# The second layer's head: x added to the latent products by PE, sigmoids from PSUM, and copies by ACT in place of DVE's sums

## What is computed

```python
base = sigmoid(r) * (num / maximum(den, 1e-8)); out = base * (0.8 + 0.2 * tf)     # r is x
...
x_lat = x @ fc1_w.T                                       # layer 0: 32 small experts in a space of 128
h = relu2(einsum('tl,eil->eti', x_lat, w1)) * cw.T[:, :, None]
routed = einsum('eti,eli->tl', h, w2) @ fc2_w.T
...                                                       # out = shared + routed
X1_q = rows quantized by their absmax; X2 = gelu(X1_q @ W1_q.T * scales + B1)     # layer 1
out = quantized(X2) @ W2_q.T * scales + B2
```

## Time and profile before

| | |
|---|---|
| three runs | 461.81, 463.07, 463.24 us; median 463.07 |
| the profiled execution | 462.28 us, its span 460.5 us |
| busy, share of the span | PE 89%, PEld 57%, DVE 72%, ACT 53%, POOL 52% |
| mean granted clock of PE | 0.974 |
| 181 to 199 us | end of layer 0's experts, head of layer 1 |
| 199 to 229 us | layer 1's loop over 8 tiles |
| 235 to 247 us | routing of layer 2 |
| 254 to 401 us | layer 2's 23 blocks of experts |

### The profile page before, as it was taken

One profiled execution on the slowest core, in us unless ns is written; L12 is line 12 of the kernel. 1 busy time (PEld: TensorE's weight loads), 2 busy tenths in 40 slices (PEclk: granted clock), 3 DMA queues, 4 the chain that ended last, 5 costly groups with the idle time before them and its releaser, 6 DMA issues.

```text
span 460.5 us, 6031 instructions
## 1 busy us (share of the span) xinstructions
PE 408.4 (89%) x1734; PEld 261.8 (57%) x1741; DVE 329.3 (72%) x621; ACT 243.5 (53%) x486; POOL 240.8 (52%) x339
## 2 busy tenths in 40 slices
PE   7798999999899999777765999999999999985795
PEld 7576787555455556445632456665556666652553
DVE  5997789999999998899765277547547311028995
ACT  6534682667667667568963132333323232328884
POOL 5473036686789995232003457866775454204642
PEclk9999999999999999979995799999999999999999
DMA  7900006356555543000025878898899986050011
GB/s 227 407 11 0 1 1 227 128 189 221 184 200 171 216 168 137 1 1 2 1 91 174 319 273 289 297 370 288 331 343 311 311 305 216 31 186 0 13 36 46
DMA packets 23664, 77.39 MB, mean 168 GB/s; under 512 B 3440, under 2 KB 7920, under 8 KB 20176
## 3 DMA queue, kind: packets, MB, share of 16 engines
q1 hardware_dynamic: 20336, 69.94, 42.7%
q0 software_dynamic: 2208, 6.03, 4.3%
q10 hardware_dynamic: 1088, 1.05, 0.7%
HBM read 71.76 MB, written 5.24 MB: 167 GB/s over the span
## 4 chain that ended last, share of the span: by engine, by line
PE 35%; issue 5%; DVE 4%; ACT 4%; DMA 3%; POOL 1%; ACTq 0%; POOLq 0%; DVEq 0%
PE bank L1957 18%; PE bank L1977 10%; PE bank L1968 2%; DVE gl L1543 2%; PE bank L1940 1%; DMA gy<-y_rows 1%; PE bank L1827 1%; DMA xb<-cond_rows,row_i 1%; DVE pt L1550 1%; PE bank L1808 1%; PE bank L1819 1%; ACT q2T L838 1%; POOL st L623 1%; DMA y_rows<-yb,dest_i 1%; ACT gl L830 0%
## 5 line engine op out<-in xcount | busy, mean ns | idle before, releaser
L1957 PE MATMUL bank<-gu,xbT 128*128 128x512 f32 x184 | 86.0, 612 | 0.9 <-ACT xbT L903 0.9
L1739 PE MATMUL bank<-hx,w2raw 128*128 128x512 f32 x128 | 67.2, 607 | 4.2 <-DVE hx L1278 3.3
L1479 DVE TENSOR_TENSOR hm<-bank,sl 128x512 f32<-128x512 f32 x23 | 15.9, 692 | 71.3 <-PE bank L1957 40.3
L781 ACT ACTIVATE rl<-bank 128x512 f32<-128x512 f32 x64 | 38.1, 595 | 37.9 <-PE bank L1586 37.1
L1957 PEld LDWEIGHTS bank<-gu,xbT 128*128 128x128 f32 x184 | 35.6, 196 | 37.2 <-issue 34.7
L559 POOL DMA_INDIRECT xb<-cond_rows,row_i x23 | 26.1, 1134 | 54.1 <-DVE row_i L1429 36.7
L1584 PE MATMUL bank<-xlhi,w1hi 128*128 128x512 f32 x64 | 49.4, 771 | 0.0
L1977 PE MATMUL bank<-dn,hT 128*128 128x256 f32 x184 | 45.2, 388 | 3.5 <-ACT hT L914 0.7
L1278 DVE TENSOR_TENSOR hx<-bank,cwb 128x512 f32<-128x512 f32 x64 | 42.0, 659 | 4.8 <-ACT bank L785 4.7
L566 POOL DMA_INDIRECT y_rows<-yb,dest_i x23 | 25.1, 1093 | 35.5 <-ACT yb L920 34.4
L1075 DVE RECIPROCAL fw<-fw 128x256 f32<-128x256 f32 x24 | 41.5, 1731 | 0.0
(11 more groups left out here) (304 smaller groups left out, 914.9 us busy)
## 6 DMA issues: line engine op xcount, KB each, us to landing
gu<-in_gu SPq DMA_DIRECT2D x22, 1024.0 KB
cwb<-cw_rows SPq DMA_DIRECT2D x32, 512.0 KB, 4.1
dn<-in_dn SPq DMA_DIRECT2D x23, 512.0 KB, 4.5
traw<-in_t SPq DMA_DIRECT2D x3, 1024.0 KB
w1raw<-in_w SPq DMA_DIRECT2D x8, 256.0 KB, 4.7
w2raw<-in_w SPq DMA_DIRECT2D x8, 256.0 KB, 4.5
kT<-in_kt SPq DMA_DIRECT2D x4, 256.0 KB, 4.5
x<-in_x SPq DMA_DIRECT2D x2, 512.0 KB, 6.5
```

What stands on the lines that cost most here:

```text
L781: act.activation(rl[:, u % 3, :], bank[u % 4][:], ACT.Relu).then_inc(sem("r_ready"), 1)
L1739: pe.matmul(bank[4 + s][:], w2raw[:, e // 4 % 2, e % 4, :], hx[:, 0, u % 4, :], start=(e == 0), stop=(e == E0 - 1), skip_group_check=True) ...
L1957: ins = pe.matmul(bank[2 * (b % 2) + up][:], xbT[:, b % 2, k, :], gu[:, b % RING, k, up * I2:up * I2 + I2], start=(k == 0), stop=(k == KC ...
```

## The change

- PE: each latent product is preceded by a product of the identity with the x tile in the same bank, which the latent product then adds to. The bank holds the new x.
- ACT: the sigmoid is taken pair by pair from PSUM, and the bank is then copied to x. For half 0 both copies follow the sigmoids, ahead of `latent_copy(1)`. For half 1 both stand behind the load of Gelu's table and ahead of `l1_gelu(0)`.
- DVE: `add_routed` is gone, four sums of 512 columns. `make_cond` of layer 1 waits for its own pair's sigmoid.
- `x1_ready` now comes from ACT's copies. POOL's bias sums wait for it rather than for the sigmoids.

```diff
-                pool.wait_ge(sem("sig_ready"), 2 + t // TH + 1)
+                pool.wait_ge(sem("x1_ready"), t // 2 + 1)
...
+            def sigmoid_routed(v):
+                act.wait_ge(sem("fo_ready"), v + 1)
+                act.activation(cond[:, 2 * v:2 * v + 2, :], latent_bank(v)[:].rearrange("p (t c) -> p t c", t=2), ACT.Sigmoid
+                               ).then_inc(sem("sig_ready"), 1)
+
+            def copy_routed(v):
+                act.activation(x[:, 2 * v:2 * v + 2, :], latent_bank(v)[:].rearrange("p (t c) -> p t c", t=2), ACT.Copy
+                               ).then_inc(sem("x1_ready"), 1)
...
             load_table(5, ACT.Sigmoid)
-            sigmoid_x(1, (0,))
+            sigmoid_routed(0)
+            sigmoid_routed(1)
+            copy_routed(0)
+            copy_routed(1)
             latent_copy(1)
...
             l1_first(0)
-            sigmoid_x(1, (1,))
+            sigmoid_routed(2)
+            sigmoid_routed(3)
             l1_first(1)
             load_table(1, ACT.Gelu_apprx_tanh)
+            copy_routed(2)
+            copy_routed(3)
             l1_gelu(0)
...
-                    dve.wait_ge(sem("sig_ready"), 2 * l + b // 2 + 1)
+                    dve.wait_ge(sem("sig_ready"), 2 + b + 1 if l else b // 2 + 1)
...
-            add_routed(0)
-            add_routed(1)
...
             row_scales(0)
-            add_routed(2)
-            add_routed(3)
...
-                        ins = pe.matmul(latent_bank(v)[:, half * C:half * C + C],
-                                        ylat[:, s, t * P:t * P + P], fc2w[:], start=True, stop=True)
+                        out = latent_bank(v)[:, half * C:half * C + C]
+                        pe.matmul(out, ident[:], x[:, 2 * v + half, :], start=True, stop=False)
+                        ins = pe.matmul(out, ylat[:, s, t * P:t * P + P], fc2w[:], start=False, stop=True)
```

More of the change, by code:

```diff
@@ L683, in side_exp, with sigmoid_x @@
                 act.activation(ekk[:, 2 * b:2 * b + 2, 1, :], kT[:, 2 * b:2 * b + 2, :], ACT.Exp).then_inc(sem("ek_raw"), 1)
[L685 to L690, removed]
+            def sigmoid_routed(v):
[5 more added lines that the diff above has]
+                               ).then_inc(sem("x1_ready"), 1)
+            def sigmoid_x():
+                for s in range(2):
+                    act.wait_ge(sem(f"x_in{s}"), 16)
                     act.activation(cond[:, TH * s:TH * s + TH, :], x[:, TH * s:TH * s + TH, :],
@@ L744, in _ @@
                 first_exp(2 * b + 1)
-            sigmoid_x(0)
+            sigmoid_x()
             act.wait_ge(sem("consts"), 5)
@@ L1265, in weight_scale @@
                 chain(dve.tensor_scalar(ws[:, 4:6], ws[:, 2:4], 1.0 / (Q * Q), None, ALU.mult))
[L1267 to L1270, removed]
             def expert_h(u):
```

## The result

| | before | changed |
|---|---|---|
| executions | 11 | 11 |
| median | 460.93 us | 464.56 us |
| lowest to highest | 460.05 to 463.24 | 462.07 to 468.33 |
| the profiled execution, its span | 462.28, 460.5 us | 462.23, 460.5 us |
| mean granted clock of PE in it | 0.974 | 0.984 |

The ratio is 1.0065, 95% interval 1.0033 to 1.0096: slower by 3.0 us (1.5 to 4.4); the medians lie 3.6 us apart. The forecast was +3.35 us.

The account below looks back on a forecast made before the run. DVE was taken to set the pace in layer 1, with PE close behind. PE's identity products (+2.80 us) and the wait on a copy (about +0.55) gave +3.35 on a 463.07 us median: 466.4 us, range 464.2 to 468.2.

Parts of the forecast that it names:

- The sum: Layer 1, up to xp(1): 2.80 us from identity products plus about 0.55 from the wait on a copy, +3.35; chance 0.59.
- turn of quantized rows: PE's turn behind the second half's latent products: starts at 193.21 instead of 190.41 us, +2.80.
- the third copy: ACT's first copy of half 1, behind Gelu's table load: starts at 197.19 us, ends at 197.79.
- second upward product: PE's product into bank 2, which waits for the third copy: starts at 197.84 us and takes 1.04.
- xp(1): DVE's step behind the second upward product: starts at 198.90 us instead of 195.55, +3.35.
- Rival (b): Identity products run at the turns' rate, 0.86 us a half instead of 1.71: +1.64, 464.7 us; chance 0.09.
- PE's room: PE's slack ahead of the turn of quantized rows in the kernel before: 0.6 us, no more.
- Rival (a): PE's low clock falls on the second upward product, 0.85 us more on the path: 467.3 us; chance 0.16.
- Rival (c): PE's extra products are hidden, the copy still holds the second upward product: no change, 463.2 us; chance 0.08.
- Rival (d): DVE's relief from 2.5 us of sums counts, neither PE nor the third copy last: -1.6, 461.5 us; chance 0.05.
- Rival (e): ACT's table switch takes one more load of 1.28 us, all behind 4.63 later: 467.7 us; chance 0.03.
- D: From half 0's first latent product to DVE's first l1_scales, 16.61 us before; forecast for that end: 3.35 us later.

Follow-up runs that it names:

- no_identity: The changed kernel without its eight identity products, the sum with the old x left out: D 16.84 us, single time 461.05 us.
- the four runs: Changed kernel without identity products, with them doubled, with half 1's copies ahead of Gelu's table load, without products plus early copies: D 16.84, 23.54, 19.00, 15.74 us.
- the filler: Kernel before plus 32 products into an unread bank, in PE's gaps of layer 2's routing: 459.85 us, ratio 0.9969.

## Why the prediction was right and where it failed

**The step that failed is the base.** The sum was put on "the median of the three runs (463.07)", with 0.8 us of room for it, the distance of one execution from that median. Eleven executions of the kernel before have a median of 460.93, 29 and 20 others 461.02 and 461.06: the base was 2.1 us too high, more than twice its room. 460.93 + 3.35 is 464.3, and 464.56 was measured, 1.8 below the forecast of 466.4; the ratio put on 460.93 gives 463.9, below my low end of 464.2. There was bad luck in it, since all three executions lie above the median of the eleven. But they had already spread over 1.4 us, as the text itself said, and I left that out of the range. Where the time can move was in the trace as well: the profile has a low clock from 242 to 259 us, over block 0's products. I read the clock at 197 to 208 us, where the change is, and not where it costs most.

**The sum itself**, against the changed kernel's rows (whose first latent product starts 0.06 later):

| step | forecast | measured |
|---|---|---|
| identity products, a half | +1.71 us | 1.73 us |
| second half starts | 189.79 | 189.87 |
| turn of quantized rows | 193.21 | 193.43 |
| DVE's waits for the gain, the first and the second xp | 3.2, 0.6; 2; 1.0 | 3.26, 0.48; 2.12; 1.00 |
| the third copy starts | 197.19 | 197.38 |
| second upward product | 197.84 | 198.01 |
| xp(1) | 198.90 | 199.09 |
| first l1_scales | 202.0 | 202.21 |
| given back in layer 1 or the routing | nothing | 0.28 us (3.49 to 3.21) |

The price of an identity product came from a row of the same form in layer 0 and held to 0.01 us. Rival (b) fell with it. PE's room was read too large: the text says 0.6 us, but the row of the turn has 0.34. The 1.71 us for four latent products leaves out that the first one behind the wait takes 0.54 us and not 0.43 (189.87 to 190.41 in the changed kernel). That is most of the 0.14 us between 3.35 and 3.49. Rival (a) did not happen in this execution: the clock fell 0.8 us behind the end of the critical product, at the next one, and DVE's work covered that. Rival (c) was a price of +0.15 if PE cost nothing: no_identity measured +0.23. Rival (d) has DVE's relief at -1.6; with everything else out of the way it is -0.87, since PE is next. Rival (e), a longer switch of tables, has no trace: 1.40 us from the start of the load, as taken. By the Trainium skill's 2.66 us (ScalarE: Activation LUTs, What ACT_TABLE_LOAD costs) the copy would have started at 198.6 and not at 197.38; the measurement decides.

The split of the sum, 2.80 us to PE and 0.55 to the copy, holds as a path: the turn of rows came 2.96 later and the rest added 0.53. It is not what each part costs. By the four runs the identity products cost 3.26 us and the place of the copies 1.10, and DVE's relief, of which the text said that it "buys nothing", takes 0.87 off. The three add up to the path's 3.49, which is why the forecast of D is near though none of its terms is the price of its part.

## What to carry to other kernels

Work moved off the engine that sets the pace is only worth what the next engine's room allows, and that room is read from the same timeline: here DVE had none, PE 0.3 us, and 3.4 us of products were put on it. Before moving a sum to another engine, look for work of the busy engine that belongs elsewhere in time: moving one reciprocal into its waits, with the sigmoids in pairs, brought 0.86 us at that place. And when a change is smaller than the spread of executions, measure it between two landmarks of the trace, look at a third one further on (of that 0.86 us, 0.40 was left there), and take the base from as many executions as the result.

## What the runs showed beyond that

- The granted clock behind a gap of PE makes a difference of 2.8 us in eight products of a 460 us kernel from one trace to the next, and hides a change of 3.5 us in one pair of profiles. 32 products into an unread bank, in gaps that were there anyway, brought 0.3% (0.1 to 0.5%).
- With the filler PE was busy for 3.75 of 4 us from 236 to 240 and for 3.81 from 240 to 244, and the clock still fell for some 3 of the 4 us from 248 to 252 (0.62 granted, between 0.50 and 1.00). What PE did just ahead were the short routing products (24 columns). Which of them let the clock fall was not tried.
